# Five groups in flight instead of four in the group stage of a fused convolution, attention and mixture-of-experts kernel

## The chip, the cores and the metric

One NeuronCore of one Trainium2 chip runs the whole program. Its engines each take their own instructions in the order in which they are written, and meet at semaphores: PE (TensorE, matrix products, with its weight loads shown as PEld), DVE (VectorE), ACT (ScalarE), POOL (GpSimd) and SP, which here issues DMAs. The metric is the device time of one execution in microseconds (us), and the number to be predicted is the median of such runs.

## What is computed

The input is 32 images of 64 channels and 16 x 16 pixels, in fp32. In outline, with the residual sums of the reference:

```python
x = x + conv_block(_gn(x))            # group norm over channel pairs; 3x3 depthwise; "y + bias + x"
t = _to_tokens(x)                     # 8192 tokens of 64 channels
t = t + attn(_ln_t(t))                # LSH attention and an MLP
t = t + moe(_ln_t(t))                 # top 2 of 8 experts
return _from_tokens(t, x)

# conv_block: softmax over an axis of length 1 makes every 3x3 weight 1
wt = jax.nn.softmax(wt, axis=1)
# attn: keys and values are means over 4 hashes x 8 buckets of the image's tokens
buckets = jnp.argmax(concatenate([rotated, -rotated], axis=-1), axis=-1)
pooled = pooled / sum_buckets
attn = softmax(where(mask, q @ k * scale, -big)); x = x + attn @ v
y = layer_norm(x, norm2_g, norm2_b)
return x + gelu(y @ fc1_w + fc1_b) @ fc2_w + fc2_b
# moe: softmax router, top 2, gates normalised, silu(h1) * h3, down projection
topk_probs, topk_idx = jax.lax.top_k(probs, TOP_K)
```

## The kernel before

The program has two stages and a short end. The **group stage** takes the 32 images in NG = 8 groups of GB = 4 images, that is 1024 tokens, and does everything up to the router. Its result for each group is 2048 rows of 130 floats (each token twice, once for each chosen expert) that POOL scatters to a DRAM table `expert_rows`, sorted by expert, in 16 indirect DMAs a group. The **expert stage** walks 71 tiles (NT) of 256 rows of that table, with the weights of one expert each; its first tile can be loaded only when the last scatter of the last group has landed. The end sums the two results of each token and stores.

The group stage is a software pipeline written by hand. Every step of a group is a small function (`convolution`, `rotate`, `scores`, `fc1`, ...), and each engine has one function `iteration(a, b, c, d, late)` that lists its steps for one **round** in the order in which the engine runs them; `pipeline`, near the end of the file, calls it with `a=i, b=i-1, c=i-2, d=i-3, late=i-4`. So in one round stage a of one group runs beside stage b of the group before it, and so on. No scheduler changes that order; an engine that reaches an instruction whose semaphore isn't there waits, and everything behind it waits too. Where one buffer serves several groups, further waits keep them apart.

The stages in the kernel before: **a** is the group norm statistics (`channel_statistics`, `channel_variances`, `pair_statistics`), the convolution, which is a horizontal sum of three on DVE (`row_sums`, into `hsum`) and four PE products with the identity for each quarter of the tokens (`convolution`, L531 and L533, two halves `s`), the first layer norm (`centre1`, `squares1`, `variance1`, `token_rstd`, `normalise1`) and the turning of `n1` (L543). **b** is the attention: `rotate` (L550), `queries` (L557), `buckets`, `bucket_sums`, `bucket_means`, `turn_pooled`, `store_pooled` (L1021), `keys_values`, `key_value_blocks`, four pieces of `scores` (L593) with `centre_scores` (L1037 and L1039), `exponentials`, `turn_prob` (L601), `store_prob` (L788), `attend` (L611) and `attended` (L1049), and the residual. **c** is the MLP: `turn_n2`, `fc1` (L629), `gelus` (L803), `fc2` (L637), `centre3`, and the next layer norm. **d** is the router: `router`, `centre_logits`, `picks` in two halves (first and second choice), `places` and `row_places` (the destination rows, L1140). **late** is the scatter (L473) of a group whose places were found a round before. POOL also computes every reciprocal root with `pow`: `group_rstd` (L431), `token_rstd` (L435), `late_rstd` (L440), and three sums over a whole 128 x 512 tile: `token_sum` (L445), `unit_sum` (L451), `residual` (L457).

PSUM has eight banks. In this stage bank 0 holds the statistics, the convolved tokens and the turned `n1`; banks 1 and 2 (`bk12`) the scores, and also the logits and the places; banks 3 and 4 (`bk34`) queries, keys, values and turned probabilities; bank 5 the rotations, pooling and attended values; bank 6 the turned `n2` and `wtok` and half of fc1; bank 7 the other half of fc1 and fc2. The second and third layer norm share `cent_c`, `sq_c`, `vare_c` and `rc`.

## Time and profile before

| | us |
|---|---|
| median of 3 runs | 896.84 |
| lowest and highest | 896.77 and 897.52 |
| the profiled execution, its own time | 899.25 |
| its span, first to last instruction | 897.4 |

| engine | busy us | share of the span |
|---|---|---|
| PE | 696.8 | 78% |
| DVE | 504.8 | 56% |
| ACT | 327.3 | 36% |
| POOL | 363.8 | 41% |

The profile is of one execution. The group stage fills it from the start to about 518 us, when the last scatter goes out; the expert stage begins at 523 us and ends near 877 us. In the rows of the trace, "busy" is time in which an engine executed something; the bracket behind a row gives the idle time of the engine just before it, and what ended it. PEclk is the granted TensorE clock as a share of full speed: 1.00 is 2.4 GHz and 0.50 is 1.2 GHz. A view by windows gives for each stretch the busy time of each engine and the clock. The view by line or tile gives mean times; the timeline lists single instructions, with neighbours of one line merged ("x8").

### The profile page before, as it was taken

What the parts mean: (1) busy time and instruction counts of PE and PEld (TensorE: products, weight loads), DVE (VectorE), ACT (ScalarE), POOL (GpSimd) and SP (SyncE); (2) the same over time, 40 slices, a digit from 0 to 9 for tenths busy, and PEclk for the clock granted to TensorE, in tenths of its full rate; (3) what the DMA queues carried; (4) which work ended last, traced back from release to release, by engine and by line L of the source; (5) the groups of instructions that cost most, each with busy time, mean ns of one, the idle gap of its engine ahead of it and who ended that gap; (6) DMA issues with size and microseconds to landing.
All of it is one profiled execution on the core that took longest, in us unless ns stands there. A gap on an engine that the chain in (4) does not pass through costs nothing.

```text
span 897.4 us, 13860 instructions
## 1 busy us (share of the span) xinstructions
PE 696.8 (78%) x4632; PEld 526.3 (59%) x4632; DVE 504.8 (56%) x1246; ACT 327.3 (36%) x597; POOL 363.8 (41%) x353
## 2 busy tenths in 40 slices
PE   3577879697777968779560069999999999999970
PEld 3365767566565755657440047677677777777750
DVE  2366575775866668564523025655655655656644
ACT  0132424324242432333320034555555555555530
POOL 1213040453718366380747603343443443443440
PEclk9575857657585765755555579999999999999995
DMA  2000000010100000010004434556565555555517
GB/s 76 0 13 1 13 0 12 1 43 6 34 22 27 22 19 30 4 42 4 30 24 98 132 103 143 155 166 171 153 172 173 146 174 161 163 175 171 171 34 281
DMA packets 46615, 75.47 MB, mean 84 GB/s; under 512 B 7488, under 2 KB 30048, under 8 KB 46544
## 3 DMA queue, kind: packets, MB, share of 16 engines
q1 hardware_dynamic: 34512, 57.12, 21.5%
q0 software_dynamic: 8640, 12.74, 4.3%
q10 hardware_dynamic: 3392, 4.73, 1.5%
q8 instruction: 37, 0.61, 0.3%
q14 instruction: 34, 0.28, 0.1%
HBM read 58.54 MB, written 16.47 MB: 84 GB/s over the span
## 4 chain that ended last, share of the span: by engine, by line
PE 48%; issue 22%; POOL 19%; DVE 6%; DMA 3%; ACT 1%; POOLq 0%; SPq 0%; ACTq 0%; DVEq 0%
PE bk L715 22%; POOL expert_rows L473 14%; PE bk L726 11%; PE bk L703 3%; PE bk L533 2%; PE bk L733 2%; POOL rr L435 2%; DMA srow<-expert_results 1%; PE bk L611 1%; PE bk L593 1%; POOL x2t L457 1%; PE bk L637 1%; PE bk L557 1%; PE bk L550 1%; PE bk L531 1%
## 5 line engine op out<-in xcount | busy, mean ns | idle before, releaser
L1204 DVE TENSOR_TENSOR units<-bk,silu 128x512 f32<-128x512 f32 x213 | 147.4, 692 | 179.6 <-ACT silu L872 156.0
L499 POOL DMA_INDIRECT expert_results<-yout,xin x142 | 139.7, 984 | 218.0 <-DVE yout L1215 190.6
L715 PE MATMUL bk<-xs,wbuf 64*128 64x256 f32 x1704 | 205.3, 388 | 1.1 <-ACT xs L859 1.1
L715 PEld LDWEIGHTS bk<-xs,wbuf 64*128 64x128 f32 x1704 | 160.4, 188 | 44.6 <-issue 25.8
L872 ACT ACTIVATE silu<-bk 128x512 f32<-128x512 f32 x213 | 127.2, 597 | 87.1 <-PE bk L715 74.3
L473 POOL DMA_INDIRECT expert_rows<-srow,pos x128 | 131.7, 1029 | 39.5 <-issue 39.5
L726 PE MATMUL bk<-units,wbuf 128*64 128x256 f32 x852 | 107.6, 388 | 0.0
L440 POOL TENSOR_TENSOR rc<-vare_c,c_mhalf 128x8 f32<-128x8 f32 x16 | 27.7, 1732 | 174.9 <-DVE vare_c L1062 174.9
L611 PE MATMUL bk<-vblk,prob_t 128*128 128x72 f32 x256 | 49.3, 356 | 39.7 <-DVE att L1049 31.9
L726 PEld LDWEIGHTS bk<-units,wbuf 128*64 128x64 f32 x852 | 54.8, 136 | 32.4 <-issue 11.7
L611 PEld LDWEIGHTS bk<-vblk,prob_t 128*128 128x128 f32 x256 | 45.5, 264 | 47.0 <-issue 33.3
L703 PE MATMUL bk<-const,xin 128*128 128x128 f32 x142 | 31.3, 303 | 43.8 <-DMA xin<-expert_rows 43.8
L1037 DVE TENSOR_REDUCE smax<-bk 128x16 f32<-128x512 f32 x32 | 22.0, 688 | 59.4 <-PE bk L593 59.4
L703 PEld LDWEIGHTS bk<-const,xin 128*128 128x128 f32 x142 | 14.3, 141 | 67.1 <-issue 67.1
L859 ACT ACTIVATE xs<-bk 128x256 f32<-128x256 f32 x71 | 27.1, 381 | 67.5 <-PE bk L703 67.5
L864 ACT ACTIVATE ysb<-bk 128x256 f32<-128x256 f32 x71 | 27.3, 384 | 63.2 <-PE bk L726 63.2
L788 ACT ACTIVATE prob_t<-bk 128x512 f32<-128x512 f32 x32 | 18.3, 593 | 61.4 <-PE bk L601 61.4
L803 ACT ACTIVATE hid<-bk,fc_bias 128x512 f32<-128x512 f32 x32 | 20.3, 684 | 48.6 <-PE bk L629 45.5
L637 PEld LDWEIGHTS bk<-small,hid 128*128 128x128 f32 x256 | 35.9, 227 | 2.0 <-ACT hid L803 1.8
L435 POOL TENSOR_TENSOR rr<-vare_a,c_mhalf 128x16 f32<-128x16 f32 x8 | 23.4, 2919 | 33.6 <-DVE vare_a L987 33.4
L593 PE MATMUL bk<-kblk,qt 65*128 65x256 f32 x128 | 36.9, 425 | 0.1
L637 PE MATMUL bk<-small,hid 128*128 128x64 f32 x256 | 36.1, 310 | 0.3 <-ACT hid L803 0.3
(181 smaller groups left out, 1038.9 us busy)
## 6 DMA issues: line engine op xcount, KB each, us to landing
wbuf<-in_weights SPq DMA_DIRECT2D x71, 576.0 KB
xin<-expert_rows SPq DMA_DIRECT2D x71, 130.0 KB
expert_results<-yout,xin POOLq DMA_INDIRECT x142
xg<-in_x SPq DMA_DIRECT2D x8, 256.0 KB
expert_rows<-srow,pos POOLq DMA_INDIRECT x128
srow<-expert_results SPq DMA_DIRECT2D x8, 256.0 KB, 5.3
srow<-expert_results ACTq DMA_DIRECT2D x8, 256.0 KB, 6.1
out<-t ACTq DMA_DIRECT2D x8, 256.0 KB, 5.6
```

The costliest lines, as they stand in the source:

```text
L435: g.tensor_tensor(rr[:, :, :].rearrange("p a j -> p (a j)"), vare_a[:, :, :].rearrange("p a j -> p (a j)"), c_mhalf[:, :], ALU.pow).then_i ...
L440: g.tensor_tensor(rc[:, :], vare_c[:, :], c_mhalf[:, 0:NJ], ALU.pow).then_inc(rc_ready, 1)
L473: g.indirect_dma_start(rows[0:NE * REG, :], bass.IndirectOffsetOnAxis(ap=pos[:, d, k, j:j + 1], axis=0), srow[:, d % ROW_SLOTS, k, j, :], ...
L499: g.indirect_dma_start(results[:, :], bass.IndirectOffsetOnAxis(ap=xin[:, t % X_SLOTS, h, ROW - 1:ROW].bitcast(U32), axis=0), yout[:, t % ...
L593: last = mm(bk12[:, p % 2, bp * 256:(bp + 1) * 256], qt[:, j * P:(j + 1) * P], kblk[:, m, :, :].rearrange("c h m -> c (h m)"), start=True, ...
L611: last = mm(av_ps[:, 2 * (p % 2) + bp, :], prob_t[:, p % 2, 2 * bp + ch, :], vblk[:, m, ch, :], start=ch == 0, stop=ch == 1)
L637: last = mm(y_ps[:, 2 * q + par, :], hid[:, a, par, q * P:(q + 1) * P], fc2_s[:, a, :], start=a == 0, stop=a == 1)
L703: last = turn(xt_ps[:, h * P:(h + 1) * P], xin[:, t % X_SLOTS, h, 0:2 * C], ident)
L715: last = mm(bank[:, ch * MT:(ch + 1) * MT], wbuf[part, t % W_SLOTS, at:at + P], xs[part, t % 2, :], start=True, stop=True)
L726: last = mm(yt_banks[t % 2][ch * C:(ch + 1) * C, 0:MT], wbuf[:, t % W_SLOTS, at:at + C], units[:, t % 2, q, ch * MT:(ch + 1) * MT], start= ...
L872: f(silu[:, q, :], h1_ps[q], ACT.Silu).then_inc(silu_ready, 1)
L1204: tt(units[:, t % 2, q, :], h3_ps[q], silu[:, q, :], ALU.mult).then_inc(unit_ready, 1)
```

## The change

The pipeline has five stages a to e and NG + 4 rounds. Stage **a** now ends with the first half of the convolution; **b** has the second half, the first layer norm, rotations, queries, buckets, keys, values and the first two pieces of the scores; **c** the other scores and the attention; **d** the MLP, the router and the first choice; **e** the second choice and the places. The lists of ACT stand one letter later than those of the other engines for the same work, since its list begins in the middle of theirs.

Beside the order, these things change. Each layer norm has its own buffers (`cent1` to `cent3` and so on), and `u` and `u_tok` have two slots. The logits and places move from banks 1 and 2 to banks 6 and 7, the values from bank 3 to bank 4. The normalised image and its residual are written by ACT (`normalise_x`, `add_x`) instead of DVE, for which POOL computes three more tiny operations in `group_rstd`. The key blocks are written by ACT in eight copies (`key_blocks`) instead of four DVE products. `variance1` loses four small DVE instructions, the first choice is taken from the logits less their maximum, and a few pairs of small instructions become one. POOL issues 5 of a group's 16 scatters in one piece and the other 11 in a second piece of the next round.

```diff
@@ PSUM
-        v_ps = bk34[:, 0, 256:512].rearrange("p (b c) -> p b c", b=GB)
+        v_ps = bk34[:, 1, 0:256].rearrange("p (b c) -> p b c", b=GB)
-        l_ps = bk12[:, :, 0:NJ // 2 * NE].rearrange("p a (q e) -> p a q e", e=NE)
-        pos_ps = bk12[:, 1, 0:NE * NJ].rearrange("p (e j) -> p e j", e=NE)
+        l_ps = bk67[:, :, 0:NJ // 2 * NE].rearrange("p a (q e) -> p a q e", e=NE)
+        pos_ps = bk7[:, 64:64 + NE * NJ].rearrange("p (e j) -> p e j", e=NE)
@@ POOL
             def group_rstd(a):
-                g.tensor_tensor(grstd[:, :], gvar[:, :], c_mhalf[:, 0:2], ALU.pow).then_inc(grstd_ready, 1)
+                g.tensor_tensor(grstd[:, :], gvar[:, :], c_mhalf[:, 0:2], ALU.pow).then_inc(pool_step, 1)
+                g.tensor_scalar(rstd_1[:, :], grstd[:, :], 1.0, None, ALU.add).then_inc(grstd_ready, 1)
+                g.tensor_tensor(gshift[:, :], gneg[:, :], grstd[:, :], ALU.mult).then_inc(pool_step, 1)
+                g.tensor_scalar(shift_b[:, :], gshift[:, :], bias2, None, ALU.add).then_inc(grstd_ready, 1)
@@ PE
             def convolution(a, s):
                 pe.wait_ge(conv_ready, a + 1)
+                pe.wait_ge(xres_ready, 2 * a + 2)
             def scores(b, p):
                 if p == 0:
-                    pe.wait_ge(blk_ready, b + 1)
-                if p == 1:
-                    wait(pe, pos_ready, b - 1)
+                    pe.wait_ge(kblk_ready, b + 1)
             def fc1(c, a):
-                pe.wait_ge(n2t_ready, c + 1)
-                wait(pe, t2_ready, c)
+                if a == 0:
+                    pe.wait_ge(n2t_ready, c + 1)
+                    wait(pe, pos_ready, c)
             def router(d):
                 pe.wait_ge(wt_ready, d + 1)
-                wait(pe, ssub_ready, min(4 * (d + 2), 4 * NG))
+                pe.wait_ge(t2_ready, d + 1)
@@ ACT
+            def normalise_x(a):
+                act.wait_ge(grstd_ready, 2 * a + 2)
+                    f(xpad[:, s, 1:HH + 1, 1:WW + 1], xg[:, a % 2, s, :, :], ACT.Identity, bias=gshift[:, s:s + 1],
+                      scale=grstd[:, s:s + 1]).then_inc(xn_ready, 1)
+            def add_x(a):
+                    f(xres[:, s, :, :], xg[:, a % 2, s, :, :], ACT.Identity, bias=shift_b[:, s:s + 1],
+                      scale=rstd_1[:, s:s + 1]).then_inc(xres_ready, 1)
+            def key_blocks(b):
+                act.wait_ge(k_ready, b + 1)
+                for h in range(HEADS):
+                    ins = f(kblk[:, :, h, :], k_of, ACT.Copy, scale=head_of[:, h:h + 1])
...
+                run(c, exponentials, 0)
+                run(d, store_n2t)
+                run(b, store_tokens)
+                run(c, exponentials, 1)
+                run(d, gelus, 0)
+                run(c, store_prob, 0)
+                run(b, squares1)
+                run(c, store_prob, 1)
+                run(d, gelus, 1)
+                run(c, exponentials, 2)
@@ DVE
             def row_sums(a):
-                dve.wait_ge(grstd_ready, a + 1)
-                    ins = v.tensor_scalar(xpad[:, s, 1:HH + 1, 1:WW + 1], xg[:, a % 2, s, :, :], gmean[:, s:s + 1],
-                                          grstd[:, s:s + 1], ALU.subtract, ALU.mult)
-                    ins = v.scalar_tensor_tensor(out=xres[:, s, :, :], in0=xg[:, a % 2, s, :, :], scalar=bias2,
-                                                 in1=xpad[:, s, 1:HH + 1, 1:WW + 1], op0=ALU.add, op1=ALU.add)
+                dve.wait_ge(xn_ready, 2 * a + 2)
-            def key_value_blocks(b):
+            def value_blocks(b):
-                    tt(kblk[:, m, :, :], k_ps[:, M * m:M * (m + 1)].unsqueeze(1).broadcast_to([C + 1, HEADS, M]),
-                       wide(head_of, M), ALU.mult)
             def variance1(a):
-                done(v.reciprocal(vrec[:, :], vare_a[:, 0, :]))
-                done(tt(uvar[:, :], v64[:, :], vrec[:, :], ALU.mult))
@@
-    for i in range(NG + 3):
-        stages = dict(a=i, b=i - 1, c=i - 2, d=i - 3, late=i - 4)
+    for i in range(NG + 4):
+        stages = dict(a=i, b=i - 1, c=i - 2, d=i - 3, e=i - 4)
```

**PE, from the pooled keys to the second fc2 product of a round.** L577 and L580 (after: L598 and L604) are keys and values, L531 and L533 (L552 and L554) the convolution, L659 and L660 (L689 and L690) the places, L629 (L658) fc1, L593 (L614) scores, L619 (L647) the turned `n2`. Before:

```order
L577 MATMUL bk<-pooled_t,k_aug 65x128
L580 MATMUL bk<-v_aug,pooled_rep 128x64 x4
L659 MATMUL bk<-picked,const 128x64
L660 MATMUL bk<-passed,const 128x64
L629 MATMUL bk<-n2t,fc_s 128x512 x2
L531 MATMUL bk<-const,xres 128x128
L533 MATMUL bk<-const,hsum 128x128 x3
L531 MATMUL bk<-const,xres 128x128
L533 MATMUL bk<-const,hsum 128x128 x3
L629 MATMUL bk<-n2t,fc_s 128x512 x2
L593 MATMUL bk<-kblk,qt 128x256 x4
```

After:

```order
L598 MATMUL bk<-pooled_t,k_aug 65x128
L604 MATMUL bk<-v_aug,pooled_rep 128x64 x4
L552 MATMUL bk<-const,xres 128x128
L554 MATMUL bk<-const,hsum 128x128 x3
L552 MATMUL bk<-const,xres 128x128
L554 MATMUL bk<-const,hsum 128x128 x3
L647 MATMUL bk<-const,n 128x128 x4
L614 MATMUL bk<-kblk,qt 128x256 x4
L689 MATMUL bk<-picked,const 128x64
L690 MATMUL bk<-passed,const 128x64
L552 MATMUL bk<-const,xres 128x128
L554 MATMUL bk<-const,hsum 128x128 x3
```

The places and fc1 now stand behind the first scores, and the scores before the second half of the convolution. The rows that follow in the new list are the rest of that half, then fc1, one piece of scores, eight turned probabilities, another piece, fc1, eight attend products and fc2.

**POOL, one whole round.** L473 (L496) is the scatter, `rc` (`r2`, `r3`) and `rr` the roots of the layer norms, `x2t` and `u_tok` the sums. Before:

```order
L445 TENSOR_TENSOR u_tok<-tok,small 128x512
L473 DMA expert_rows<-srow,pos 67584x130 x3
L451 TENSOR_TENSOR u_tok<-u_tok,u 128x512
L431 TENSOR_TENSOR grstd<-gvar,c_mhalf 128x2
L473 DMA expert_rows<-srow,pos 67584x130 x7
L440 TENSOR_TENSOR rc<-vare_c,c_mhalf 128x8
L473 DMA expert_rows<-srow,pos 67584x130
L435 TENSOR_TENSOR rr<-vare_a,c_mhalf 128x16
L473 DMA expert_rows<-srow,pos 67584x130 x5
L457 TENSOR_TENSOR x2t<-u_tok,att 128x512
L463 IOTA srow 128x16
L440 TENSOR_TENSOR rc<-vare_c,c_mhalf 128x8
```

After:

```order
L445 TENSOR_SCALAR shift_b<-gshift,small 128x2
L480 TENSOR_TENSOR x2t<-u_tok,att 128x512
L457 TENSOR_TENSOR r2<-vare2,c_mhalf 128x8
L496 DMA expert_rows<-srow,pos 67584x130 x11
L451 TENSOR_TENSOR rr<-vare1,c_mhalf 128x16
L486 IOTA srow 128x16
L496 DMA expert_rows<-srow,pos 67584x130 x5
L462 TENSOR_TENSOR r3<-vare3,c_mhalf 128x8
L473 TENSOR_TENSOR u_tok<-u_tok,u 128x512
L467 TENSOR_TENSOR u_tok<-tok,small 128x512
L440 TENSOR_TENSOR grstd<-gvar,c_mhalf 128x2
```

The 16 scatters are in two pieces, one on each side of `rr`, and both sums of `u_tok` stand together ahead of `grstd`.

**DVE, between the pooled tile and the second pair of scores.** `smax` and `ssub` are `centre_scores`, `picked` and `passed` belong to the second choice, `pos` to the places. After:

```order
L1173 TENSOR_TENSOR picked<-oh 128x8x8
L1174 TENSOR_TENSOR gsum<-pk 128x8
L1176 SCALAR_TENSOR_TENSOR passed<-const,picked 128x72
L1179 TENSOR_SCALAR gsum<-gsum 128x8
L1180 RECIPROCAL grec<-gsum 128x8
L1182 TENSOR_TENSOR srow<-pk,grec 128x16
L1087 TENSOR_REDUCE smax<-bk12 128x16
L1089 TENSOR_TENSOR ssub<-bk12,smax 128x512
L1188 COPY picked<-passed 128x8
L1189 TENSOR_TENSOR posall<-bk67,const 128x64
```

Before, in the same place:

```order
L1126 TENSOR_TENSOR srow<-pk,grec 128x8 x2
L957 TENSOR_SCALAR xpad<-xg,gmean,grstd 128x16x16 x2
L962 TENSOR_TENSOR hsum<-xpad 128x2x256
L964 SCALAR_TENSOR_TENSOR xres<-xg,small,xpad 128x256 x2
L968 TENSOR_TENSOR hsum<-hsum,xpad 128x2x256
L1132 COPY picked<-passed 128x8
L1133 TENSOR_TENSOR posall<-bk12,const 128x64
```

The row sums, half as long, have gone ahead of both choices, and the first scores stand between the second choice and the places.

## Rows read from the trace of the kernel before

**Rows 1.** Windows: us, busy of PE, PEld, DVE, ACT, POOL, clock, DMA; two rounds.

```profile
230.00:335.00 105.00, 82.16 (x446) 65.69 (x446) 72.01 (x194) 36.47 (x60) 55.27 (x49) 0.66 0.07 24
```

**Rows 2.** Windows inside one round, and in the last rounds: the clock.

```profile
246.00:248.00 2.00, 1.98 (x7) 0.75 (x4) 1.90 (x8) 0.74 (x2) 1.70 (x2) 0.50 0.27 62
...
250.00:252.00 2.00, 2.00 (x9) 1.14 (x10) 0.56 (x2) 0.92 (x2) 0.00 (x0) 1.00 0.04 10
...
266.00:268.00 2.00, 0.00 (x0) 0.00 (x0) 1.83 (x9) 0.00 (x1) 0.27 (x1) 0.50 0.00 0
```

```profile
416.00:420.00 4.00, 4.00 (x20) 3.91 (x20) 0.00 (x0) 0.00 (x0) 0.00 (x0) 0.50 0.00 0
```

**Rows 3.** Waits from 230 to 335 us: who waited for whom, total, times, longest.

```profile
POOL rc L440 <- DVE vare_c L1062: 38.0, 2, 19.6
...
DVE smax L1037 <- PE bk L593: 13.0, 4, 4.3
...
PE bk L611 <- DVE att L1049: 9.8, 2, 4.9
```

**Rows 4.** Line 1021, the pooled tile, once a round; durations, first and last start.

```profile
L1021 DVE COPY pooled_t<-bk x8: 286/286/286, 47.1 to 398.9; 66x128 f32<-66x128 f32 x8
```

**Rows 5.** Timeline, half clock: start, us, engine, line (convolution, fc1, queries, scores, fc2).

```profile
194.18 0.50 PEld L531 LDWEIGHTS bk<-const,xres 128*128 128x128 f32 x2 [1.50 <-DVE hsum L968]
...
197.73 0.30 PEld L629 LDWEIGHTS bk<-n2t,fc_s 64*128 64x128 f32 x4
...
232.80 3.65 PE L557 MATMUL bk<-n1t,q_aug 65*65 65x512 f32 x4
```

```profile
409.16 3.06 PEld L593 LDWEIGHTS bk<-kblk,qt 65*128 65x128 f32 x8 [1.66 <-DVE vblk L1029]
...
412.31 7.16 PEld L637 LDWEIGHTS bk<-small,hid 128*128 128x128 f32 x32
```

**Rows 6.** Timeline, full clock: convolution half from 252.59, fc2 from 254.48.

```profile
252.59 0.41 PEld L531 LDWEIGHTS bk<-const,xres 128*128 128x128 f32 x2
...
254.48 3.65 PEld L637 LDWEIGHTS bk<-small,hid 128*128 128x128 f32 x32
```

**Rows 7.** Groups from 230 to 335 us: busy, mean ns of one, idle before.

```profile
L473 POOL DMA_INDIRECT expert_rows<-srow,pos x32 | 34.0, 1062 | 8.8 <-issue 8.8
...
L440 POOL TENSOR_TENSOR rc<-vare_c,c_mhalf 128x8 f32<-128x8 f32 x5 | 8.4, 1672 | 38.0 <-DVE vare_c L1062 38.0
...
L435 POOL TENSOR_TENSOR rr<-vare_a,c_mhalf 128x16 f32<-128x16 f32 x2 | 5.9, 2936 | 0.1
...
L1039 DVE TENSOR_TENSOR ssub<-bk,smax 128x512 f32<-128x512 f32 x8 | 5.5, 692 | 0.3
...
L803 ACT ACTIVATE hid<-bk,fc_bias 128x512 f32<-128x512 f32 x8 | 5.1, 683 | 12.5 <-PE bk L629 12.5
...
L803 ACT ACT_TABLE_LOAD x2 | 2.6, 1283 | 0.0
...
L774 ACT ACTIVATE pooled_rep<-pooled_t 65x128 f32<-65x128 f32 x8 | 1.8, 297 | 7.8 <-DVE pooled_t L1021 7.8
```

**Rows 8.** Timeline: a DVE product beside a POOL sum, and alone.

```profile
231.13 1.27 POOL L445 TENSOR_TENSOR u_tok<-tok,small 128x512 f32<-128x512 f32 x1
231.18 1.77 DVE L1066 TENSOR_TENSOR n<-cent_c,rc 128x512 f32<-128x512 f32 x1 [0.93 <-POOL rc L440]
```

```profile
442.44 0.69 DVE L1066 TENSOR_TENSOR n<-cent_c,rc 128x512 f32<-128x512 f32 x1 [1.28 <-POOL rc L440]
```

**Rows 9.** Timeline, end of the group stage: last places, last scatter.

```profile
479.76 0.22 DVE L1140 CAST pos<-posf 128x16 uint32<-128x16 f32 x1
```

```profile
517.50 0.96 POOL L473 DMA_INDIRECT expert_rows<-srow,pos  x1 [0.31 <-issue]
```

**Rows 10.** Timeline: two small chained DVE instructions.

```profile
241.56 0.22 DVE L1100 TENSOR_TENSOR peq<-prest,pk 128x64 f32<-128x64 f32 x1
...
241.82 0.22 DVE L1101 TENSOR_TENSOR peq<-peq,const 128x64 f32<-128x64 f32 x1
```

456 lines of the change are left out of this document (244 added, 212 removed).

## The prediction

> **What bounds the kernel now.** I read the windows first. Two rounds of the group stage take 105 us, and in them no engine is full: PE is busy 82.16 us, DVE 72.01, POOL 55.27, ACT 36.47 [rows 1]. So a round of some 52.5 us is bounded by engines that wait for one another in turn. The waits name the places [rows 3]: PE's attend products wait for DVE to have read the last ones (4.9 us a round in one piece), DVE waits for scores, and POOL sits 19 us in front of one tiny root while its scatters queue behind it. The second thing to see is the clock. PE's 82.16 us are at a mean of 0.66 of full speed [rows 1]. In a round it stands at 0.50, rises once after the products of fc1 and the convolution came without a gap (0.50 at 246 to 248, 1.00 at 250), and falls in a stretch in which PE is idle (266 to 268) [rows 2]. Third, the pooled tile is stored once a round, first at 47.1 and last at 398.9 us [rows 4]: I use it as the mark from which rounds are counted. Seven rounds take 351.8 us, 50.3 each. Fourth, the end: the last places are there at 479.8, but the last scatter starts at 517.5 [rows 9], since POOL still had the group before to scatter. Everything behind that is not touched by the change: 899.25 - 518.5 = 380.75 us in the profiled execution, its 1.85 us around the span included.
>
> **The change, part by part.** *Work moved.* DVE loses two writes of half a tile each for the normalised image and the residual, four key products, and about six small instructions: some 4.5 us of 36 a round, taking 0.69 for a full tile [rows 7] and 0.26 for a small chained one [rows 10] as measures. ACT gains what DVE lost, about 3.5 us on its 18. POOL gains three instructions on two columns, at most 0.3 each. PE's work is the same. The new bounds of a round are then DVE about 32, POOL about 32 (16 scatters at 34.0 + 8.8 over 32 = 1.34 us make 21.4; roots 1.67 twice and 2.94 [rows 7]; the sums 1.27 three times [rows 8]) and PE, whose work depends on the clock: 41 us at 0.66, so 27 at full clock and 54 at half, if all of it scaled.
>
> *The walk of a new round.* I walk from one mark (the pooled tile stored, time 0) to the next, with PE at half clock at first. Prices of PE at half clock: half a convolution 3.55 (194.18 to 197.73), one piece of scores 1.57 (two from 409.16 to 412.31), queries 3.65 [rows 5]; at full clock half a convolution 1.89 and fc2 3.65 [rows 6], against 7.16 [rows 5].
> - ACT makes the repeated pooled tile (four, 0.91), the residual (0.8) and eight key blocks (1.85, by the spacing of the first four): scores could start at 3.7. PE does the values to 2.8, half a convolution to 6.35, the turned n2 to 7.25, and the first scores to 8.8. DVE uses that time for row sums, first and second choice (25 small steps), to 7.0. It then waits to 9.3: first scores centred 10.75.
> - PE: second scores 10.4, places 11.5, second half of the convolution 15.05. DVE: places 13.35, second scores 14.8, value blocks 15.55. The tokens reach it from ACT at 16.1: centred 17.55, **the first place where PE at half clock sets the pace**.
> - ACT now is in the way: an exponential 16.7, a table load 1.28 and two GELUs of 0.68 [rows 7] to 19.3, one copy, then the squares at 20.5. DVE has the variance at 21.45, POOL the root at 24.5, normalised tiles 26.1. Behind the second GELUs (22.4) PE does fc2, at full clock, to 26.1, DVE centres it to 28.6, and ends the third variance at 30.2.
> - ACT's copies of the turned n1 stand behind the squares of the third norm: second half at 31.4. Rotations 34 at mixed clock, buckets 36.6, queries 38.2, turned wtok, bucket sums, router 41.5, pooled tile stored **43**.
>
> *Collisions.* Where DVE multiplies two SBUF tiles while POOL sums a tile, it takes 1.77 instead of 0.69 us [rows 8]. In the new order the two sums of u_tok and one root stand beside centre2, normalise3 and the row sums: 0 to 5 us a round, and I take 3, near the two such delays of a round before. That agrees with "SBUF — State Buffer" of the Trainium skill (section "SBUF: two separate sides"), by which DVE and GpSimd take one shared pair of ports as an exclusive lock. By its further rule, that a DVE instruction in a two-port mode also keeps GpSimd from writing descriptors, scatters would get dearer as DVE gets denser; beside DVE products a scatter starts every 1.34 us on average here [rows 7], so I add nothing.
>
> *POOL's queue.* After the second root (at about 2) come 11 scatters, 14.7 us, then rr: ready for it at 17, needed at 21.45. Then rr, 5 scatters, r3: 21.45 + 2.94 + 6.9 = 31.3, plus 1.67 = 33, needed at 34. Both just fit; the wait of 19 us in front of a root is gone, since the scatters stand in it.
>
> *The sum.* Steady round 43 + 3 = 46. The first mark comes at 44.9 instead of 47.1 (the root's input loses three small steps and r12, the group root gains 0.7). Round 1 has no MLP and router: 35. Round 2 no second choice: 43. Then five of 46: last mark at 44.9 + 35 + 43 + 230 = 353 instead of 399, **46 us less**. The last rounds, of one or two groups, are chains at half clock of the same steps, and give the last places 82 us behind the mark as against 80.9. But of the group before only 11 scatters are left then, and with 16 of its own they end at mark + 106; before it was 119.6. **That is 13.6 more**. Together 59.5 us: 839.8 in terms of the profiled execution. That lay 2.4 us above the median, so 837.3.
>
> **The rivals.** *The clock stays up the whole round.* In the walk no gap of PE is above 1 us at full clock, where today one of 4.9 goes before the fall [rows 3]. Then the walk has no half-clock stretch: PE 27 of 38 us, DVE sets the pace with 35 + 3. Rounds 34, 37 and five of 38: last mark 306, 47 us less than forecast: 790. "TensorE: Matmul & The Clock Gate" of the Trainium skill (section "Why this matters for your kernels") says that continuous work brings full speed and only idle gaps between bursts of products take it away; by that rule this is the forecast. Rows speak against it: from 416 to 420 PE was busy all 4.00 us at 0.50, behind fc2 products with small outputs [rows 2], so what PE does counts, and rotations, router and pooling follow in a row here. 8%.
>
> *The clock rises in only some rounds.* The convolution's halves were 3 us apart on either side of scores and fc1, and now stand apart by turned n2, scores and places, 6 us. A round of mostly half clock costs 51 to 54: 862 to 884. 11%.
>
> *The clock never rises, and the kernel is slower.* The rise came at the end of fc1, half a convolution and fc1 in one row [rows 2]. If the new neighbours of each half never release it, PE needs up to 54 us a round plus the gaps at places, GELUs and centring that nothing fills, some 2.5: 56.5. Rounds 37, 54 and five of 56.5: last mark at 418.5, 19.5 later than now, less 13.6 in the scatters: 6 us more, **903**. It decides from 55.5 us a round upward. 4%.
>
> *The change doesn't do what it says.* The walk would have to miss a wait that takes the place of the old one, for instance squares1 behind the GELUs at an even later time, or rr behind 11 scatters, so that a round stays 52 to 53: the rounds before gain nothing but the scatters, 880 to 897. 4%, of which 2 within 0.2% of no change.
>
> **How the numbers follow.** The forecast is a rise in nearly every round, 41 to 51 us a round by the bounds of the collisions and of where the clock rises: 812 to 862, chance 73%, value 837. For 8 in 10 I go from 803 to 872, which takes in the upper part of the full-clock case and half of that in which some rounds fail. Faster by over 0.2% (1.8 us, about what a measurement of this kernel can tell): 0.93; within it 0.02; slower 0.05.
>
> **What would show it.** Right: the pooled tile about every 46 us, last at 353; PE busy about 85 to 90% of a steady round with the clock at 0.6 to 0.7; the wait of POOL for vare_c gone; last scatter 106 us behind the last mark. A mark every 38 us at clock 1.00 shows the first rival, every 55 at 0.50 the third. Wrong otherwise: if the wait ends at sq1 or rr in every round with PE idle, my prices on ACT or POOL's queue failed; if DVE's instructions are mostly long beside POOL's, the collisions.

## The result: 797 us, below the range

The kernel after the change takes **797.15 us** in the median of 4 runs (793.79 to 802.02), beside 897.18 us for the kernel before: a ratio of 0.889, 95% interval 0.883 to 0.895. The forecast was 837 us with a range of 803 to 872, so it was too slow by 40 us. The sign and, within 1.4 us, the first two marks were right; the length of a full round was not. The four runs lie at 793.8, 793.9, 800.4 and 802.0 us, and the traced one is the longest of them; where the 8 us between them lie is said below, at the drain.

The profiled execution took 802.02 us, with a span of 800.2. Its slices of the page are, by engine, then the granted clock:

```profile
PE   2597989998989996967206999999999999999960
PEld 1475768685868684665104776777777777777730
DVE  2356577788777878442402666555556555555645
ACT  1142637374646464422203554555554455555420
POOL 2203150777676777546660333344443334444340
PEclk9765778787869696555557999999999999999995
```

Slices 2 to 16 are the rounds. PE's digits there are mostly 9 and 8, and no engine has a stretch of low digits. Two rounds in windows (columns as in [rows 1]: us, busy of PE, PEld, DVE, ACT, POOL, clock, DMA):

```profile
159.24:237.04 77.80, 71.24 (x446) 57.13 (x446) 61.97 (x159) 43.97 (x84) 57.11 (x56) 0.79 0.11 35
```

The same 446 products of [rows 1] now take 71.24 us instead of 82.16, and they fill 92% of the time. The clock is 0.79 instead of 0.66. The mark, the pooled tile stored once a round, is now line 1073 (durations, first and last start), against [rows 4]:

```profile
L1073 DVE COPY pooled_t<-bk x8: 274/276/288, 46.0 to 314.9; 66x128 f32<-66x128 f32 x8
```

The eight marks are at 46.04, 81.36, 120.39, 159.24, 197.50, 237.04, 275.63 and 314.90 us. So the rounds are 35.3, 39.0, and then 38.9 on average over the last five, where 35, 43 and 46 were forecast:

| | forecast | measured | difference |
|---|---|---|---|
| first mark | 44.9 | 46.0 | +1.1 |
| round 1 | 35 | 35.3 | +0.3 |
| round 2 | 43 | 39.0 | -4.0 |
| five steady rounds | 230 | 194.5 | -35.5 |
| last mark to end of last scatter | 106 | 106.0 | 0 |
| everything behind it | 380.75 | 381.1 | +0.4 |

Nearly the whole miss is in the rounds that have all stages: 35.5 us in the five steady ones and 4.0 in the one before them. The waits from 150 to 310 us, four rounds (who waited for whom, total, times, longest), show what the change removed and what is left:

```profile
ACT wtok_t L871 <- PE bk L674: 21.8, 4, 5.9
...
POOL grstd L440 <- DVE gneg L1012: 11.7, 4, 2.9
PEld bk L674 <- DVE wtok L1137: 10.6, 5, 5.0
...
DVE smax L1087 <- PE bk L614: 7.3, 4, 2.8
...
DVE wtok L1137 <- POOL r L462: 6.0, 5, 1.6
```

POOL's waits of 19 us in front of a root [rows 3] are gone. The longest wait that remains for PE's instructions is that of the turned wtok (line 674) for DVE's product of the third norm (line 1137).

### The profile page after: what moved, and what is told of

The parts are those of the page before. It is cut to its first block, busy times and chain, and to the rows that moved or that the text cites. A ratio compares the mean times of both kernels' runs of the same rounds, so it can differ in the third digit from the quotient of the medians.

```text
span 800.2 us, 13984 instructions
## 1 busy us (share of the span) xinstructions
PE 662.7 (83%) x4632; PEld 500.1 (62%) x4632; DVE 467.0 (58%) x1094; ACT 353.5 (44%) x693; POOL 366.6 (46%) x377
## 3 DMA queue, kind: packets, MB, share of 16 engines
q1 hardware_dynamic: 34512, 57.12, 24.5%
## 4 chain that ended last, share of the span: by engine, by line
PE 43%; POOL 5%; issue 4%; DMA 2%; DVE 1%; ACT 0%; POOLq 0%; ACTq 0%; SPq 0%
PE bk L748 25%; PE bk L759 12%; POOL expert_rows L496 5%; PE bk L736 3%; PE bk L766 2%; DMA srow<-expert_results 2%; DMA expert_rows<-srow,pos 0%; POOL expert_results L519 0%; DMA xin<-expert_rows 0%; DMA expert_results<-yout,xin 0%; DVE t L1281 0%; POOL x2t L480 0%; DVE hid L1285 0%; POOLq L64 0%; ACT silu L934 0%
## 5 line engine op out<-in xcount | busy, mean ns | idle before, releaser
L496 POOL DMA_INDIRECT expert_rows<-srow,pos x128 | 128.9, 1007 | 44.2 <-issue 38.0
L451 POOL TENSOR_TENSOR rr<-vare,c_mhalf 128x16 f32<-128x16 f32 x8 | 23.4, 2922 | 70.6 <-DVE vare L1037 70.6
L639 PEld LDWEIGHTS bk<-vblk,prob_t 128*128 128x128 f32 x256 | 34.8, 218 | 6.7 <-ACT prob_t L846 4.8
L614 PE MATMUL bk<-kblk,qt 65*128 65x256 f32 x128 | 37.3, 431 | 0.0
L639 PE MATMUL bk<-vblk,prob_t 128*128 128x72 f32 x256 | 36.7, 305 | 0.0
L554 PE MATMUL bk<-const,hsum 128*128 128x128 f32 x192 | 36.4, 343 | 0.0
L839 ACT ACTIVATE prob<-ssub 128x512 f32<-128x512 f32 x32 | 19.4, 626 | 37.7 <-DVE ssub L1089 37.6
L554 PEld LDWEIGHTS bk<-const,hsum 128*128 128x128 f32 x192 | 33.9, 260 | 0.0
```

Source lines behind the costliest of these rows:

```text
L496: g.indirect_dma_start(rows[0:NE * REG, :], bass.IndirectOffsetOnAxis(ap=pos[:, d, k, j:j + 1], axis=0), srow[:, d % ROW_SLOTS, k, j, :], ...
L554: last = mm(o, hsum[:, s, h0 + dy:h0 + dy + 8, :], ident, start=False, stop=dy == 2)
L614: last = mm(bk12[:, p % 2, bp * 256:(bp + 1) * 256], qt[:, j * P:(j + 1) * P], kblk[:, m, :, :].rearrange("c h m -> c (h m)"), start=True, ...
L639: last = mm(av_ps[:, 2 * (p % 2) + bp, :], prob_t[:, p % 2, 2 * bp + ch, :], vblk[:, m, ch, :], start=ch == 0, stop=ch == 1)
```

## One round of after, beside the forecast walk

I take the round from 197.50 us, so that 197.50 is time 0 of the walk. Windows of two microseconds around the clock's rise and fall (us, busy of PE, PEld, DVE, ACT, POOL, clock, DMA):

```profile
202.00:204.00 2.00, 2.00 (x11) 2.00 (x11) 1.67 (x9) 1.62 (x2) 1.70 (x2) 0.50 0.29 101
204.00:206.00 2.00, 2.00 (x9) 1.82 (x8) 0.00 (x0) 0.00 (x0) 1.39 (x3) 0.50 0.14 42
206.00:208.00 2.00, 2.00 (x13) 1.78 (x13) 1.31 (x3) 0.00 (x0) 1.66 (x2) 0.93 0.20 67
...
226.00:228.00 2.00, 2.00 (x15) 2.00 (x14) 1.66 (x5) 0.63 (x1) 1.97 (x2) 0.69 0.10 33
228.00:230.00 2.00, 2.00 (x5) 0.90 (x6) 1.12 (x1) 0.00 (x0) 2.00 (x2) 0.50 0.04 12
```

The clock goes from 0.50 to full at 206.3, that is 8.8 us behind the mark, while PE makes the first scores. The walk had it at half clock until the second half of the convolution was done, at 15.05; it is done at 12.2, at full clock. In the five steady rounds the rise comes 5.7 to 8.8 us behind the mark, at different products of the same order: in the first half of the convolution, in the turned n2 or in the first scores.

The kernel before had its rise at that distance too, 7.6 to 10.1 us behind the mark in its last five full rounds. The round with the mark at 241.11 is the one of [rows 2]; its row for 250 to 252 shows full clock, but not since when:

```profile
248.00:249.00 1.00, 1.00 (x8) 1.00 (x7) 0.96 (x5) 0.52 (x1) 0.69 (x2) 0.65 0.81 266
248.70:250.00 1.30, 1.30 (x13) 1.18 (x12) 1.30 (x5) 0.00 (x0) 0.59 (x1) 1.00 0.27 89
```

The rise came at 248.7, while PE made half a convolution, and the second piece of fc1 began only at 249.92. So the prediction's reading, that it came at the end of fc1, was 1.2 us too late and at the wrong product.

The traces also give the price of a late rise, within one order of instructions. In the kernel after and two more traces of it on other chips, all with the same instructions in the same order, a steady round whose rise comes 5.7 us behind its mark takes 38.0 us, 6.1 goes with 38.3, 6.7 with 38.5, 7.4 with 38.8, 8.6 and 8.8 with 39.5 (the last round before the drain, with less work in it, is left out). That is 0.5 us of round for each us of delay. Drawn on to 15.05, an estimate, a round would take 42.7 us.

The timeline shows what follows in the round from 197.50 (start, us, engine, line):

```profile
211.95 0.69 DVE L1025 SCALAR_TENSOR_TENSOR cent<-ssum,tok 128x512 f32<-128x512 f32 x1
...
215.75 0.16 DVE L1037 TENSOR_SCALAR vare<-ssq 128x8 f32<-128x8 f32 x1
...
216.00 2.93 POOL L451 TENSOR_TENSOR rr<-vare,c_mhalf 128x16 f32<-128x16 f32 x1 [2.52 <-DVE vare L1037]
...
225.60 2.56 PE L571 MATMUL bk<-rot_aug,n1t 65*128 65x32 f32 x16
...
228.40 3.65 PE L578 MATMUL bk<-n1t,q_aug 65*65 65x512 f32 x4
228.83 1.25 POOL L473 TENSOR_TENSOR u_tok<-u_tok,u 128x512 f32<-128x512 f32 x1
228.88 3.00 DVE L1137 TENSOR_TENSOR wtok<-cent,r 128x512 f32<-128x512 f32 x1 [1.11 <-POOL r L462]
...
230.05 1.28 POOL L467 TENSOR_TENSOR u_tok<-tok,small 128x512 f32<-128x512 f32 x1
...
234.10 0.69 PE L587 MATMUL bk<-n,onehot 128*32 128x65 f32 x16 [1.05 <-DVE onehot L1059]
```

Tokens are centred at 15.1 (walk 17.55), the first variance is there at 18.4 (21.45), its root at 21.4 (24.5), the rotations end at 30.7 (34), the queries at 34.5 (38.2). The lead over the walk is 2.8 us at the end of the convolution, and that is the clock's: PE needed 4.8 us for first scores, places and that half, and the walk 7.8 at half clock. It is 3.7 us at the queries; what added the rest was not separated. Then DVE's product takes 3.00 us beside two POOL sums, where it took 1.77 beside one [rows 8], and the buckets behind it keep PE waiting. But the mark still comes 5.0 us behind the end of the queries, and not 4.8 + 3.

## The experiments

All experiments are edits of the kernel after. Rounds are given as the mean of the last five.

**The queue of POOL.** The forecast had rr "ready at 17, needed at 21.45" behind 11 scatters. This run takes those 11 out of the rounds, and does them behind the group stage.

```
 # POOL, in a round
-                run(e, scatter, 5, 5)
-                run(e, scatter, 10, 6)
 # POOL, behind the last round
+            for d in range(NG):
+                ...
+                scatter(d, 5, 11)
```

> The kernel after, with 11 of the 16 scatters of each group taken out of the rounds and done in a row behind the last round; the first 5 stay where they are. The rows scattered late have another group's tokens in them, since only three slots of rows exist. Only the marks up to the last one are to be compared, since 88 scatters, about 112 us, now stand behind the group stage. Theory S (on a slow chip TensorE's completions are held while a long train of scatters is in flight: in the slow runs they came back 0.7 to 1.2 us behind the last packet of the train in about three of four cases): no standstill behind the marks, rounds of 37.5 to 39.5 and a last mark at 305 to 315 on either kind of chip. Theory P (the chip holds TensorE back by itself at full clock, whatever POOL does): on a slow chip rounds of 45 to 50 as in the control. On a fast chip: rounds of 38 to 39 either way, or 1 us less if POOL's queue bounds the round.

> The kernel after, unchanged, as the control of this call. By the two control runs so far a chip gives either 797 us (rounds of 38.2 to 39.5) or 837 us (rounds of 45 to 50.5 from the fourth mark on, with TensorE's semaphores standing still for 3 to 6 us once a round).

Measured: the control 794.22 us, marks from 45.9 to 313.6; without the 11 scatters marks from 46.7 to 312.7, and 893.07 us with the 88 late ones. A round of it, two windows:

```profile
157.59:195.56 37.97, 34.35 (x223) 27.38 (x223) 30.84 (x80) 22.01 (x42) 17.48 (x18) 0.81 0.06 17
195.56:234.97 39.41, 36.70 (x223) 29.62 (x223) 30.86 (x80) 22.01 (x42) 17.48 (x18) 0.76 0.05 16
```

POOL is busy 17.5 us instead of 28.5, and the rounds are 38.7 instead of 39.0. The 11 scatters and their 11 us of POOL a round cost nothing that can be told. This step of the forecast holds: POOL's queue fits and sets nothing. The same kernel on two more chips gave last marks at 313.7 and 313.3.

> The kernel with 11 of the 16 scatters of each group done behind the group stage, once more, to meet a chip with the standstill. If its control shows the standstill: theory S (it hangs on the long train of scatters) rounds of 37.5 to 40 from the fourth mark on and a last mark at 305 to 315; theory P (the chip alone) rounds of 45 to 50 and a last mark near 350. If its control shows none: last mark at 313 as before (38.4 us a round), and the question stays open.

> The kernel with 11 of the 16 scatters of each group done behind the group stage, a third time. If the other kernel of this call shows the standstill in its rounds: theory S (it hangs on the long train of scatters) no standstill and a last mark at 305 to 315; theory P (the chip alone) a last mark near 350. If the other shows none: last mark at 313 as twice before.

**The collisions.** First the two sums of u_tok are taken away, all but one column.

```
-                g.tensor_tensor(u_tok[:, a % 2, :, :], tok[:, :, :], ...
+                g.tensor_tensor(u_tok[:, a % 2, :, 0:1], tok[:, :, 0:1], ...
```

> The kernel after, with POOL's two sums of u_tok cut to one column of 64. This leaves the sum of tokens and bias out of the residual, so the output differs; the order, the waits and the number of instructions stay. It asks what DVE's collisions with these sums cost on the path. Theory A (the miss of 6.5 us a round is the clock, which rises some 5.5 us earlier than in my walk; the collisions lie mostly beside the queries): the third-norm product falls from 3.00 to about 0.7 us, the router products start where the queries end, the buckets start 2.3 us earlier but the bucket sums still wait for the end of the queries: 1 to 2 us a round, last mark at 301 to 308, time 783 to 792. Theory B (the collisions cost the 3 us that I added to the path): last mark at 294, time 776. Theory C (they cost nothing): 797.

Measured: 786.58 us (784.40 to 789.82), ratio 0.875 with an interval of 0.872 to 0.877. The group of the product, and of the mark:

```profile
L1138 DVE TENSOR_TENSOR wtok<-cent,r 128x512 f32<-128x512 f32 x4 | 2.8, 704 | 4.9 <-POOL r L463 4.9
```

```profile
L1074 DVE COPY pooled_t<-bk x8: 276/277/288, 46.0 to 303.4; 66x128 f32<-66x128 f32 x8
```

The product takes 0.70 us, the last mark comes 11.5 us earlier, a round is 37.5 instead of 38.9. So the sums cost 1.4 us in a steady round, not 3 and not nothing: theory A. It is the collision and not POOL's load that costs, since POOL, relieved of 11 us a round above, changed nothing. Most of the long product lies beside the queries.

Then all work is kept, and the sums are moved to where DVE has slack (it waited 1.8 to 2.8 us for the first scores).

```
                 run(c, rstd2)
+                run(b, token_sum)
+                run(b, unit_sum)
                 run(e, scatter, 5, 5)
 ...
                 run(c, rstd3)
-                run(b, unit_sum)
-                run(a, token_sum)
```

> The kernel with POOL's two sums moved behind the root of the second norm, once more, in the hope of a chip without the standstill. On a fast chip: 785 to 791 if the collision with the third-norm product costs 1 to 1.6 us a round and is free in its new place, 797 or more if it moves along with it. On a slow chip 842 to 846 as before.

Measured: **784.91 us** (779.94 to 787.43), ratio 0.873 (0.869 to 0.877), beside 794.22 (0.885, 0.883 to 0.887) for the kernel after on the same chip. The timeline, two places of one round:

```profile
223.69 0.69 DVE L1137 TENSOR_TENSOR wtok<-cent,r 128x512 f32<-128x512 f32 x1 [1.11 <-POOL r L462]
...
231.15 1.57 POOL L467 TENSOR_TENSOR u_tok<-tok,small 128x512 f32<-128x512 f32 x1
231.47 1.33 DVE L1152 SCALAR_TENSOR_TENSOR peq<-lsub,const 128x64 f32<-128x64 f32 x1
```

The collision moves to two steps of the first choice (1.33 and 1.05 us instead of 0.22), where it hides. Rounds are 37.8 instead of 39.0, the last mark is at 305.5 instead of 313.6. By the marks it gives most of what leaving the sums out gives (303.4), and it is, with the version that moves the turned n2 below, the fastest in this study that keeps all work.

A third way leaves the sums and moves DVE: buckets and pair statistics ahead of the third-norm product, bucket sums ahead of the turned wtok, turned pooled tile ahead of the router.

```
 # DVE                                  # TensorE
+                run(b, buckets)        +                run(b, bucket_sums)
+                run(a, pair_statistics)                 run(d, turn_wtok)
                 run(d, normalise3)     -                run(b, bucket_sums)
-                run(b, buckets)        -                run(d, router)
-                run(a, pair_statistics)                 run(b, turn_pooled)
                                        +                run(d, router)
```

> The kernel after, with three swaps that keep all work: DVE makes the buckets and the pair statistics in front of the third-norm product (which waits 1.1 us for its root and then takes 3.00 us beside two POOL sums, while the rotations have been ready for 3.6 us); TensorE makes the bucket sums in front of the turned wtok, and the turned pooled tile in front of the router; DVE stores the pooled tile before it centres the logits. Theory A (this product and the collision are on the path from rotations to the mark): bucket sums start where the queries end, the mark comes 2 to 2.9 us earlier in each round of 39, last mark at 295 to 301, time 777 to 785. Theory B (the round is set by POOL's 16 scatters, roots and sums, which take 32 of 39.5 us, or by another chain): less than 1 us a round, 790 to 797.

Measured: 804.20 us (803.38 to 804.81), no gain and probably a small loss: rounds of 39.7 instead of 38.9, the last mark at 317.0 instead of 314.9 or 313.6. The rest of the difference to 797 us lies in the drain, which takes either 99 or some 106 us (see below) and took 107.7 in this trace. Its timeline at the same place:

```profile
231.14 1.25 POOL L473 TENSOR_TENSOR u_tok<-u_tok,u 128x512 f32<-128x512 f32 x1
...
231.68 2.25 DVE L1057 TENSOR_TENSOR beq<-beq,const 128x256 f32<-128x256 f32 x1
...
232.36 1.28 POOL L467 TENSOR_TENSOR u_tok<-tok,small 128x512 f32<-128x512 f32 x1
...
234.90 0.68 DVE L1137 TENSOR_TENSOR wtok<-cent,r 128x512 f32<-128x512 f32 x1
```

The collision hit another product of two SBUF operands, now one of the buckets (2.25 us instead of 0.42), which is on the path itself. My reading that the third-norm product as such was on the path fell; what costs is whichever such product meets the sums. Behind the mark the values then waited for ACT's repeated pooled tile, which stood behind the router's exponential: 4.2 us in four rounds.

**The clock's rise.** The first half of the convolution is moved from behind the values to directly in front of the second half.

```
 # TensorE
+                run(b, convolution, 0)
                 run(b, convolution, 1)
 ...
-                run(a, convolution, 0)
                 run(c, turn_n2)
```

> The kernel after, with TensorE's first half of the convolution moved from behind the values to directly in front of the second half, behind the places; all work is kept. Theory A (the clock rises at about 8.8 us behind the mark because a convolution half and the first scores stand in one row there): the rise comes later, at about 12 us behind the mark or more, the full-clock stretch of a round falls from 20.5-23.9 us to some 17, tokens come 1.5 to 3 us later in five full rounds: 805 to 818. Theory B (where the clock rises doesn't depend on this place, and the products before the tokens are the same): tokens at the same time, first scores 3 us earlier, 797 or up to 5 less.

Measured: 810.30 us (810.18 to 810.64), ratio 0.902 (0.900 to 0.904). Windows of the round whose mark is at 164.85:

```profile
172.00:174.00 2.00, 2.00 (x9) 1.73 (x7) 1.07 (x2) 0.86 (x2) 1.70 (x2) 0.50 0.21 67
174.00:176.00 2.00, 2.00 (x11) 2.00 (x11) 1.76 (x6) 0.25 (x1) 1.39 (x3) 0.50 0.18 58
176.00:178.00 2.00, 2.00 (x18) 2.00 (x18) 1.43 (x4) 0.00 (x0) 1.54 (x2) 0.91 0.13 42
```

The rise comes 11.3 to 11.6 us behind the mark in the steady rounds instead of 5.7 to 8.8, on average 4.6 us later. A round is 41.1 us instead of 38.9. The full-clock stretch is 20.5 us (it is 20.5 or 23.9 in the kernel after, and I had expected 17); it is above all the half-clock stretch that grows, from 17 to 20.6. A rise at 11.5 with a round of 40.9 is what 0.5 us for each us of delay gives, starting from 38.0 at 5.7. That is theory A with the wrong stretch named.

Why the rise comes later is less clear. The edit changes the order, but not that alone: the half convolution used to stand where the turned n2 would else wait for DVE. Without it PE is idle there, from 3.2 to 4.0 us behind the mark, in each steady round:

```profile
168.83 1.11 PE L647 MATMUL bk<-const,n 128*128 128x128 f32 x4 [0.73 <-DVE n L1117]
```

Whether the rise is held back by that gap or by the other products in front of it was not tested apart. A gap of 0.34 us at the same place in one round of the kernel with the sums moved (mark at 154.88) went with a rise at 7.0, no later than without.

The other way round, on top of the moved sums, the turned n2 goes behind the first scores, so that convolution and scores are one row:

```
                 run(a, convolution, 0)
-                run(c, turn_n2)
                 run(b, scores, 0)
                 run(b, scores, 1)
+                run(c, turn_n2)
                 run(d, places)
```

> The kernel with POOL's two sums moved (785 us on a chip without the standstill, against 794 for the kernel after), and besides TensorE's turned n2 behind the first two scores instead of in front of them. Theory A (the clock rises in the row of convolution half and scores, and the sooner this row is one piece, the sooner it rises): the rise comes up to 3 us earlier behind the mark in some rounds, rounds of 36 to 38, last mark 298 to 304, time 777 to 784. Theory B (the turned n2, 128 columns by 128 rows four times, is as dense as the scores, and the place of the rise stays): 783 to 788, the first scores being centred 0.7 us earlier where DVE waits anyway. Theory C (the row behind the scores becomes weaker and the clock falls or rises later): 790 or more. If the chip shows the standstill: 840 to 846.

Measured: 784.50 us (782.89 to 798.62), the same as with the sums moved (784.91). Rounds are 37.6, the last mark at 303.0. The rise comes 5.7 to 7.7 us behind the mark, against 5.6 to 7.9 with the sums moved alone: theory B, the place of the turned n2 does not matter here.

**The clock's fall.** With the sums moved, the queries go in front of the rotations, into the full-clock stretch.

```
+                run(b, queries)
                 run(b, rotate)
                 run(a, pair_variances)
-                run(b, queries)
```

> The kernel with the sums moved and the queries in front of the rotations, once more. On a fast chip: 775 to 782 if the queries then run at full clock, the same as with the sums moved alone if they do not, 800 or more if the later rotations hold up the buckets. On a slow chip 854 as before.

Measured: 794.85 us (793.79 to 804.63), 10 us slower than with the sums moved alone on the same chip. Timeline:

```profile
226.78 1.91 PE L579 MATMUL bk<-n1t,q_aug 65*65 65x512 f32 x4
...
228.53 2.81 PE L571 MATMUL bk<-rot_aug,n1t 65*128 65x32 f32 x16
...
231.38 0.42 DVE L1055 TENSOR_REDUCE bmax<-bk 128x32 f32<-128x256 f32 x1 [0.63 <-PE bk L571]
```

The queries do run at full clock, in 1.91 instead of 3.65 us. But now rotations run at half clock and DVE waits for them. In the steady rounds that about cancels: they take 38.3 us instead of 37.8. Most of the loss comes earlier. The first mark is at 48.1 instead of 44.8, the fourth at 161.7 instead of 154.9, the last at 313.8 instead of 305.5; in front of the first mark PE is at half clock in any case (from 36 to 44 us), so there the rotations simply come 3.65 us later.

**DVE's share.** The key blocks go back from ACT to DVE, as four products behind the row sums.

```
 # ACT
-                run(c, key_blocks)
 # DVE
                 run(a, row_sums)
+                run(b, key_blocks)
```

> The kernel after, with the key blocks back on DVE (four products behind the row sums) instead of eight copies on ACT. If DVE only fills a wait there (it waits 1.8 to 2.8 us for the first scores in a steady round): 797, within 3. If DVE sets the pace between the mark and the first scores: 1.4 us a round later, 807. If ACT, relieved of 2.1 us, lets the exponentials and the tokens come earlier: 790.

Measured: 799.72 us (793.94 to 803.91), ratio 0.888 (0.883 to 0.894), rounds of 39.0. No difference can be told. DVE waits for the first scores anyway, so in this order that move of the change is worth nothing.

**Six runs on two chips that behave otherwise.** The next four kernels ran together on one further chip, and all came out far slower:

```
 # TensorE, places first; the other three edits stand above
+                run(d, places)
                 run(b, scores, 0)
                 run(b, scores, 1)
-                run(d, places)
```

> The kernel after, with TensorE's products for the places moved from behind the first two scores to in front of them. Theory A (the clock rises in the row of convolution half, turned n2 and scores; the small places products change that row little, and DVE waits for the scores anyway): first scores 1.1 us later, tokens at the same time, rounds 38.5 to 39.5, 793 to 800. Theory B (DVE's first scores set the pace): 1.1 us a round, 805. Theory C (any weaker stretch ahead of the scores holds the rise back): the full-clock stretch comes 1 to 3 us later, rounds of 40 to 41, 805 to 812.

> The kernel after, with POOL's two sums of u_tok moved from behind the root of the third norm to behind the root of the second norm, a round later for the tokens' one: they then stand beside DVE's small steps of the first and second choice, where DVE waits 1.8 to 2.8 us for the first scores anyway. All work is kept. Theory A (the sums cost 1 to 1.6 us a round by their collision with the third-norm product, as their absence gave 11.5 us at the last mark): third-norm product 0.7 us, last mark at 303 to 309, time 785 to 791. Theory B (the collision moves along and costs the same beside the choices, or holds up the scatters and the root of the first norm): 797 to 803.

> The kernel after, with TensorE's queries in front of the rotations. In the kernel after the clock falls in the rotations, so that the queries take 3.65 us at half clock. Theory A (the queries, in the full-clock stretch, take 1.9 us; the rotations come 1.9 us later, but DVE is busy with the third-norm product until 3.6 us behind them, so the buckets come at the same time): the mark 0 to 1 us earlier a round, 790 to 797. Theory B (the longer dense row also holds the clock up for more of the round): full-clock stretches of 23.9 us or more in most rounds, 2 to 3.5 us a round, 775 to 783. Theory C (the queries run at half clock there too, so that the buckets come later): 800 to 810.

> Both edits in one: POOL's two sums behind the root of the second norm, and TensorE's queries in front of the rotations. If the clock's fall and the collision are the two things that keep the mark back at the end of a round: DVE's third-norm product and the buckets are done at 34.9 us behind the last mark instead of 36.6, TensorE's queries take 1.9 us: 2.5 to 3.5 us a round, last mark 292 to 299, time 775 to 782. If only the collision counts, the time is that of the kernel with the sums moved alone.

Measured: places first 840.76 us, sums moved 846.00, queries first 849.58, both 854.13, the kernel before 897.45 as ever. Four unlike edits with one loss of 45 to 60 us asked for a control, which ran on yet another chip:

> The kernel after itself, unchanged, on the chip of this call, as a control. The four kernels of the call before (places first, sums moved, queries first, and both) took 841 to 854 us, each with rounds of 37 to 39 us up to the fourth mark and of 45 to 54 behind it, where the full-clock stretches are cut to some 7 to 14 us, and a gap of 4 to 8 us stands in front of ACT's tokens. Theory A (that comes from those edits): 797, within 5. Theory B (it came from the chip on which that call ran, or from its state, and any kernel with this density would show it): 840 to 850 if this call gets such a chip, with the same gap.

> The kernel with POOL's two sums moved behind the root of the second norm, the same as the one run before (846 us), beside the kernel after on one chip. Theory A (the edit costs 49 us wherever it runs): 846. Theory B (the chip did it): the same time as the kernel after of this call within 12 us, and on a chip where that one takes 797, 785 to 800.

Measured: the kernel after, unchanged, **837.49 us** (836.66 to 843.57), ratio 0.934 (0.930 to 0.938); with the sums moved 842.90. So theory B: it is the chip. Rounds are 37.7 and 38.2 up to the fourth mark and then 45.0 to 50.5. Windows of the last undisturbed round and of the first disturbed one:

```profile
120.34:158.52 38.18, 34.33 (x223) 27.50 (x223) 30.85 (x81) 21.99 (x42) 15.67 (x16) 0.81 0.06 17
158.52:208.99 50.47, 43.84 (x223) 35.67 (x223) 30.15 (x80) 21.92 (x42) 29.74 (x30) 0.67 0.09 27
```

In the second, the timeline (PE's convolution half in four pieces, then what waits for it):

```profile
169.68 0.39 PE L552 MATMUL bk<-const,xres 128*128 128x128 f32 x2
...
169.90 0.83 PE L554 MATMUL bk<-const,hsum 128*128 128x128 f32 x6
...
171.75 1.13 PE L658 MATMUL bk<-n2t,fc_s 64*128 64x512 f32 x4 [1.02 <-DVE pos L1193]
...
172.81 1.13 PE L614 MATMUL bk<-kblk,qt 65*128 65x256 f32 x4
...
176.03 0.60 ACT L804 ACTIVATE tok<-bk 128x512 f32<-128x512 f32 x1 [5.79 <-remote]
```

The convolution that ACT needs is recorded as done at 170.73, but ACT gets its semaphore only at 176.03; "remote" says that no instruction ended near that moment. The trace's record of semaphores has all of PE's outstanding updates (convolution, fc1, scores, turned probabilities) come in one burst within 0.2 us, though the products are recorded as done from 170.73 to 174.38. Since the ends of products in the profile are modelled, it can't be told whether PE stood still or only its updates. ACT and DVE, then PE stand idle, and the clock falls at 177.5, after 10.2 us of full clock instead of 20.5 or more. So a standstill costs its own length and a part of the full-clock stretch: this round is 12 us longer than the one before it, with 5.8 us of standstill. Of 24 such rounds in the six runs, the burst comes 0.7 to 1.2 us behind the last packet of the 11 scatters in 19, and earlier in 5. Whether the scatters cause it is open: the kernel without them ran only on three chips on which the kernel beside it had no standstill. The kernel before does not lose time on either chip (897.45 and 898.75 us).

> The kernel after, unchanged, as the control of this call, to say what kind of chip it is: 793 to 802 us without the standstill, 836 to 844 with it.

It took 794.26 us. In all, the kernel after took 794 to 797 us on three occasions and 837 on one; two more chips ran its relatives above without the standstill. Places first and queries first alone were timed only with the standstill. Their marks can still be compared up to the fourth, where none has come yet: places first has it at 159.1 and queries first at 163.6, against 156.8 to 159.2 in four traces of the kernel after. So placing them first costs 2.3 us at most by then, and putting the queries first 4.4 or more, as in the run above.

## Why the forecast was right or wrong, point by point

- **What bounds the kernel, and that the wait of POOL goes: right.** The 19 us wait is gone, PE is busy 92% and the scatters are off the path, as the run with 11 of 16 taken out shows.
- **"I walk ... with PE at half clock at first", up to 15.05: this step failed.** The rise came 5.7 to 8.8 us behind the mark. I had read it in the old order as the end of fc1 [rows 2], and moved it along with fc1. It was not there even in the old kernel: it came in a half of the convolution, 7.6 to 10.1 us behind the mark. At 0.5 us a round for each us, the 8 us between 15.05 and the mean of 7.0 are worth 4 of the 7.1 us by which a round was forecast too long (an estimate), and about 3 of the 6.5 in the round above. The experiment with the halves together bears out the price. What sets the moment of the rise is not shown; it differs by 3 us between rounds of the same kernel.
- **Collisions, "0 to 5 us a round, and I take 3": mis-sized.** The single one was dearer than I had thought (3.00 us beside two sums, against 1.77 beside one), but it stands beside the queries. Taken away, it gave 1.4 us a steady round, 11.5 us up to the last mark. So 1.6 us of the miss are here. "SBUF — State Buffer" of the Trainium skill (section "SBUF: two separate sides"), with its exclusive lock, agrees: DVE's product starts 0.05 us behind the first sum and ends only behind the second, at 231.88 against 231.33.
- **The last leg, from queries to mark.** I had 4.8 us; without the sums it took 3.9, another 0.9 us. With the 4 and the 1.6 above that is 6.5 of 7.1 us; the rest is spread over small steps.
- **Work moved.** That ACT makes the key blocks was worth nothing. That was in the walk, which let DVE wait until 9.3 in the new order; it waited to 9.2.
- **The drain: right for the traced run.** Last mark to last scatter 106.0 us, forecast 106. But this hangs on the clock too: in both controls without the standstill PE had a full-clock stretch in the drain, and it took 98.9. One of them:

```profile
330.00:342.00 12.00, 9.67 (x78) 8.38 (x76) 6.41 (x12) 5.41 (x8) 4.67 (x5) 1.00 0.07 22
```

  In the profiled execution of after the same stretch was at 0.50, with PE busy all 12.00 us. Of the 9.1 us between these two traces (802.0 and 792.9 us) the drain has 7.1. The runs of after at 793.8 us had a mean clock of 0.831, that at 802.0 one of 0.821, so I take this stretch for their difference too, but the short kind was not traced on that chip. The drain of the median run is thus between right and 7 us too long.
- **The rival "the clock stays up the whole round": wrong in its mechanism, near in its number.** It forecast rounds of 38 and 790 us at clock 1.00. The rounds were 38.9, but at 0.76 to 0.81, with a fall in every one, so it came near by luck. In the round above the longest idle gaps of PE at full clock were 0.30 and 0.68 us, 2 to 3 us before the fall; from 226 to 230 PE was busy all 4.00 us and the clock went from 0.69 to 0.50. That rule of "TensorE: Matmul & The Clock Gate" (section "Why this matters for your kernels"), in the Trainium skill, by which idle gaps between bursts take full speed away, doesn't explain these rows unless gaps as short as 0.68 us count.
- **The range.** Its lower end came from "41 to 51 us a round by the bounds of the collisions and of where the clock rises". By the price above, 41 us with no collision stands for a rise at about 11 us, later than in any of the last rounds of the old kernel. With the rise at 5.7 the walk's 43 us become 38.3, and the time 799 us (estimates, all three); a lower end set there would have come within 2 us of the result. That 837 us is what one other chip measures is luck and no merit of the forecast: the standstill there was not in it.

## What to carry to other kernels

Find the clock's rise in the old trace to a microsecond, in several rounds, before tying it to a step. When an order is changed, walk the round with the rise at the earliest distance from the mark that the old trace shows, and at the latest place that the new order allows, and let both set the range. A collision between DVE and POOL was not moved away by reordering the DVE instruction that suffered it; moving the POOL work to where DVE waits anyway did it. Time the unchanged kernel on the same chip before believing that four unlike edits fail alike.

## What had not been expected of the hardware

- On two of the six chips of these experiments, PE's semaphore updates stand still for 3 to 10 us once a round, from the first round with a train of 11 scatters, and come in a burst in most of them. The kernel after loses 40 us of 797, the kernel before nothing.
- A DVE product of two SBUF operands that meets two POOL sums in a row waits for both (3.00 us instead of 0.69; a small one of the buckets 2.25 instead of 0.42); beside one sum a step of 0.22 us took 1.33.
- The clock's rise moves by 3 us between rounds of one kernel in which PE has the same products in the same order, and each us of it is worth 0.5 us of a 39 us round. Another place for half a convolution moved it by 4.6 us.
